# Adding a stored partial result on GpSimd, and taking a row's moments one block later

## The reference, cut to what matters

```python
S = S + eye(n)
Rf = S / S.sum(axis=1)[:, None];  Rb = S / S.sum(axis=0)[:, None]
Xf, Xb, Xa, Z = X, X, X, 0
for s in range(2):
    A = nucleus_softmax(Xa @ W1 @ W2 @ (Xa @ W3).T, p=0.9)   # row-wise top-p
    Xf = Rf @ Xf;  Xb = Rb @ Xb;  Xa = A @ Xa
    Z = Z + (Xf @ U1[s] + Xb @ U2[s] + Xa @ U3[s])
Y = X + Z
out = x + (Y - mean(Y)) / sqrt(var(Y) + 1e-5) * gamma + beta
```

## Time and profile before

| what | value |
|---|---|
| median of three runs | 2001.48 us |
| profiled execution | 1999.62 us |
| its span | 1997.6 us |
| TensorE busy | 1777.0 us (89%) |
| VectorE busy | 1634.1 us (82%) |
| ScalarE busy | 1364.9 us (68%) |
| GpSimd busy | 605.1 us (30%) |
| mean granted TensorE clock | 0.961 |

### The profile page before, as it was taken

One profiled execution on the slowest core, in us unless ns is written; L12 is line 12 of the kernel. 1 busy time (PEld: TensorE's weight loads), 2 busy tenths in 40 slices (PEclk: granted clock), 3 DMA queues, 4 the chain that ended last, 5 costly groups with the idle time before them and its releaser, 6 DMA issues.

```text
span 1997.6 us, 37487 instructions
## 1 busy us (share of the span) xinstructions
PE 1777.0 (89%) x11660; PEld 1312.2 (66%) x11660; DVE 1634.1 (82%) x3964; ACT 1364.9 (68%) x2201; POOL 605.1 (30%) x1056
## 2 busy tenths in 40 slices
PE   4999964899999999993976699999999999999997
PEld 3888832677777777773763466666666676767665
DVE  5444467899999999998864899999999999999987
ACT  5222266888888888983835568686868686777752
POOL 4000131244444444441341132324242323232330
PEclk9999976899999999997988899999999999999998
DMA  6999721454444444442433010101010101010122
GB/s 170 196 202 203 195 100 56 97 117 117 112 105 116 106 111 114 110 108 56 112 77 125 22 42 21 42 21 42 21 42 21 42 21 42 21 41 22 38 91 72
DMA packets 235345, 168.26 MB, mean 84 GB/s; under 512 B 188451, under 2 KB 220577, under 8 KB 235168
## 3 DMA queue, kind: packets, MB, share of 16 engines
q1 hardware_dynamic: 221264, 117.44, 21.6%
q0 software_dynamic: 3744, 22.14, 7.2%
q10 hardware_dynamic: 10288, 28.12, 4.2%
HBM read 107.99 MB, written 37.49 MB: 73 GB/s over the span
## 4 chain that ended last, share of the span: by engine, by line
issue 35%; DVE 21%; PE 19%; POOLq 9%; DVEq 7%; POOL 4%; DMA 2%; ACT 2%; ACTq 0%
DVE probs_t L1588 7%; DVE stats L1595 5%; POOLq L720 5%; PE lg L1165 2%; DMA probs_t<-row_scalars 2%; PE bank L1096 2%; PE bank L1095 2%; PE bank L1079 2%; PE lg L1096 2%; PE lg L1095 2%; PE bank L1200 2%; DVEq L1783 1%; DVE sorted_e L1614 1%; PE bank L1052 1%; DVEq L1612 1%
## 5 line engine op out<-in xcount | busy, mean ns | idle before, releaser
L1188 PE MATMUL bank<-both,s_tile 128*128 128x512 f16 x1352 | 302.4, 381 | 16.9 <-issue 16.9
L1257 PE MATMUL bank<-xcur,probs_t 128*128 128x256 f32 x1352 | 296.1, 379 | 0.0
L1165 PE MATMUL lg<-k_t,q_tile 64*128 64x512 f32 (+1 forms) x820 | 191.6, 568 | 96.1 <-DVE expo L1485 89.1
L1257 PEld LDWEIGHTS bank<-xcur,probs_t 128*128 128x128 f32 x1352 | 255.0, 190 | 33.6
L1188 PEld LDWEIGHTS bank<-both,s_tile 128*128 128x128 bf16 x1352 | 132.8, 98 | 166.7 <-issue 20.0
L1485 DVE TENSOR_SCALAR_CACHE_REDUCE expo<-lg 128x1024 f32 (+1 forms) x208 | 206.8, 1023 | 43.1 <-PE lg L1165 27.4
L660 POOL TENSOR_TENSOR window<-window,probs_t 128x832 f16<-128x832 f32 x104 | 215.2, 2069 | 81.1 <-ACT probs_t L937 68.6
L1165 PEld LDWEIGHTS lg<-k_t,q_tile 64*128 64x128 f32 x820 | 69.3, 192 | 178.6 <-DVE expo L1485 123.1
L868 ACT ACTIVATE expo<-expo,below_max 128x3327 f32<-128x3327 f32 x52 | 159.4, 3065 | 24.7 <-DVE below_max L1493 23.7
L699 POOL TENSOR_TENSOR aims<-found 128x2 f32<-128x2 f32 x26 | 5.1, 195 | 555.6 <-ACT found L903 555.6
L1588 DVE SCALAR_TENSOR_TENSOR probs_t<-expo,mine 128x1664 f32 (+3 forms) x54 | 156.4, 2896 | 8.4 <-issue 8.0
(11 more groups left out here) (303 smaller groups left out, 3628.6 us busy)
## 6 DMA issues: line engine op xcount, KB each, us to landing
s_tile<-s_scratch SPq DMA_DIRECT2D x28, 832.0 KB, 4.5
expo<-in_adj POOLq DMA_DIRECT2D x25, 831.8 KB, 9.7
s_tile<-s_scratch ACTq DMA_DIRECT2D x24, 832.0 KB, 4.5
s_scratch<-s_tile SPq DMA_DIRECT2D x14, 832.0 KB, 10.1
s_scratch<-probs_t SPq DMA_DIRECT2D x6, 832.0 KB, 9.3
s_scratch<-window SPq DMA_DIRECT2D x6, 832.0 KB, 9.6
q_tile<-q_scratch SPq DMA_DIRECT2D x104, 32.0 KB, 2.1
xa_scratch<-ht ACTq DMA_DIRECT2D x26, 128.0 KB, 2.2
```

The costliest lines, as they stand in the source:

```text
L1165: last = T.matmul(lg[c % 2][:, h * CHUNK:h * CHUNK + w], q_tile[b][DA * h:DA * (h + 1), :], k_all[DA * h:DA * (h + 1), s, c0:c0 + w], star ...
L1188: last = T.matmul(s_ps[:, 0:width], s_tile[b][:, k, :], moving, start=(k == 0 and part == 0), stop=(k == NT - 1 and part == 1))
L1257: last = T.matmul(kept_ps[1][:, 0:D], probs_t[:, k * P:(k + 1) * P], xcur[:, k, :], start=(k == 0), stop=(k == NT - 1))
```

## The change

GpSimd gets a new function `add_result`, which adds `y_in` to tile t's result in SBUF; a new semaphore `y_added` counts it. For all tiles but the last, TensorE no longer runs the identity product and ScalarE copies the result out without accumulating. One block later, after its second refinement, ScalarE reads the added result again with a copy that accumulates the row sum, and makes mean and squares there (`added_result`). GpSimd's order becomes: first bracket of tile t+2, centre tile t-1, add tile t. SyncE's load of `y_in` waits for `y_added` instead of `y_done[1]`. The last tile is made as before; in its block ScalarE takes the moments of tile 24 behind the copies L997. `skewed_loop` runs body 0 alone, 22 bodies in a loop, and 3 more alone.

```diff
@@ SyncE, load
-                sp.wait_ge(y_done[1], t + 1)
+                sp.wait_ge(y_added, t + 1)
                 sp.dma_start(y_in[:, :], dram_tile(y_dram, tile_of(m, b))).then_inc(y_loaded[1], DMA)
@@ GpSimd
+            def add_result(t, m, b):
+                y = tile3(y_all, tile_of(m, b))
+                pool.wait_ge(y_out[1], t + 2)
+                pool.wait_ge(y_loaded[1], DMA * (t + 1))
+                G.tensor_tensor(y, y, y_in[:, :], ALU.add).then_inc(y_added, 1)
...
-            with pool.Fori(0, NT // 2 - 1) as i:
-                for b in range(2):
-                    first_bracket(i * 2 + b + 2, i + 1, b)
-                    centre_result(i * 2 + b, i, b)
-            centre_result(NT - 2, NT // 2 - 1, 0)
+            def results(t, m, b):
+                if not (isinstance(t, int) and t >= NT - 2):
+                    first_bracket(t + 2, m + 1, b)
+                if not (isinstance(t, int) and t == 0):
+                    centre_result(t - 1, m - 1 + b, 1 - b)
+                if not is_last(t):
+                    add_result(t, m, b)
+            skewed_loop(pool, results)
@@ ScalarE, step
+                def added_result(t, m, b):
+                    A.activation(turned[:, 0:D], tile3(y_all, tile_of(m, b)), ACT.Copy, accum_out=y_sum[:, :])
+                    result_moments(m, b)
...
                     if is_last(t):
+                        act.wait_ge(y_added, t + 1)
+                        added_result(*before)
                         act.wait_ge(var_ready, 1)
...
+                    if before is not None and not is_last(t):
+                        act.wait_ge(y_added, t + 1)
                     if more:
                         refine(b, 1)
+                    if before is not None and not is_last(t):
+                        added_result(*before)
                     act.drain()
...
-                    A.activation(y, pv_ps[:, 0:D], ACT.Copy, accum_out=y_sum[:, :]).then_inc(y_out[1], 1)
-                    act.drain()
-                    A.activation(mean[:, column], y_sum[:, :], ACT.Copy, scale=-1.0 / D)
-                    act.drain()
-                    A.activation(turned[:, 0:D], y, ACT.Square, bias=mean[:, column], accum_out=var[:, column]).then_inc(y_moments, 1)
+                    if is_last(t):
+                        A.activation(y, pv_ps[:, 0:D], ACT.Copy, accum_out=y_sum[:, :]).then_inc(y_out[1], 1)
+                        result_moments(m, b)
+                    else:
+                        A.activation(y, pv_ps[:, 0:D], ACT.Copy).then_inc(y_out[1], 1)
...
-                    tiles_loop(act, step)
+                    skewed_loop(act, step)
@@ TensorE, step
-                    pe.wait_ge(y_loaded[1], DMA * (t + 1))
-                    T.matmul(pv_ps[:, 0:D], ident[:, :], y_in[:, :], start=True, stop=False)
-                    products(t, True)
+                    if is_last(t):
+                        pe.wait_ge(y_loaded[1], DMA * (t + 1))
+                        T.matmul(pv_ps[:, 0:D], ident[:, :], y_in[:, :], start=True, stop=False)
+                    products(t, is_last(t))
```

More of the change, by code:

```diff
@@ L349, in graph_layers @@
         x_added = sem("x_added")
+        y_added = sem("y_added")
         lo_ready = [sem(f"lo_ready_{n}") for n in range(2)]
@@ L379, in graph_layers @@
             (qk_out, 1),
+            (y_added, 1),
         ]
@@ L990, in first_end, with result_moments @@
                     result_out(t)
+                def result_moments(m, b):
+                    y, column = tile3(y_all, tile_of(m, b)), bass.ds(tile_of(m, b), 1)
+                    act.drain()
+                    A.activation(mean[:, column], y_sum[:, :], ACT.Copy, scale=-1.0 / D)
+                    act.drain()
+                    A.activation(turned[:, 0:D], y, ACT.Square, bias=mean[:, column], accum_out=var[:, column]).then_inc(y_moments, 1)
+                def added_result(t, m, b):
+                    A.activation(turned[:, 0:D], tile3(y_all, tile_of(m, b)), ACT.Copy, accum_out=y_sum[:, :])
+                    result_moments(m, b)
                 def step(t, m, b):
                     more = not (isinstance(t, int) and t >= NT - 2)
+                    before = None if isinstance(t, int) and t == 0 else (t - 1, m - 1 + b, 1 - b)
                     for g, (k0, n) in enumerate(P_GROUPS):
@@ L1017, in step @@
                     act.wait_ge(y_done[1], t + 2)
-                    y, column = tile3(y_all, tile_of(m, b)), bass.ds(tile_of(m, b), 1)
-                    A.activation(y, pv_ps[:, 0:D], ACT.Copy, accum_out=y_sum[:, :]).then_inc(y_out[1], 1)
-                    act.drain()
-                    A.activation(mean[:, column], y_sum[:, :], ACT.Copy, scale=-1.0 / D)
-                    act.drain()
-                    A.activation(turned[:, 0:D], y, ACT.Square, bias=mean[:, column], accum_out=var[:, column]).then_inc(y_moments, 1)
+                    y = tile3(y_all, tile_of(m, b))
+                    if is_last(t):
[3 more added lines that the diff above has]
+                        A.activation(y, pv_ps[:, 0:D], ACT.Copy).then_inc(y_out[1], 1)
                 for t in range(2):
```

## The result

The changed kernel takes 2007.69 us (median of 8 runs, 2006.23 to 2010.26) against 2001.11 us before (8 runs in the same comparison, 1999.64 to 2003.34): ratio 1.0036, 95% interval 1.0028 to 1.0045, which is 5.6 to 9.0 us slower. The forecast was 2007.4 us, slower. The profiled execution took 2007.77 us, its span 2005.7 us, 8.1 us more than before.

A forecast was written before the change was run, and what follows sets the result against it. VectorE, not the 98% busy TensorE, was taken to bound the second pass at 33.8 us a block. Blocks 0 and tail +5.9 on 2001.5 gave 2007.4 us; own range 2004.5 to 2009.5, 8 in 10 within 2001.5 to 2012.

The forecast's parts named there:

- VectorE closes the loop: Second pass: TensorE waits for VectorE's reciprocal L1785 each block, so removing the 0.43 us identity product gains 0.
- the 0.22 us of one block: TensorE's late start in the block shown, waiting for VectorE's reciprocal L1785; forecast to grow to 0.65 us.
- ScalarE's moments in the block cost nothing: Behind the second refinement: 1.46 to 1.65 us of work delays L1013 some 0.8 us, products not delayed; cost 0.
- GpSimd's addition is hidden in the blocks: Behind L738: 0.64 us, ending 0.3 us before VectorE's L1493; cost 0, bounds 0 and +0.64 a block.
- that cover: The 0.3 us between the addition's end and VectorE's L1493, called thin; the rival of collisions in each block had 0.14.
- The collision of block 24: Addition behind held-up L738 meets VectorE's small instructions before the last L1785: +0.4 us, bounds 0 and 0.64.
- The tail: After the last block: tile 24's moments come 7.3 us later, +7.7 with the collision; the end moves +5.9 us.
- It starts 1996.8 - 1990.9 = 5.9 us later than now: Program end: the last store, ready at 1992.6, waits for large stores filling all engines until 1996.8; end +5.9 us.
- on an engine that has just come free: Last store before the change: claimed to leave at 1989.9 and start about 1990.9, large stores having filled engines until 1989.1.
- The sum: Whole kernel: blocks 0, tail +5.9 us; span 2003.5, profiled execution 2005.5, median 2007.4.

The follow-up runs named there:

- e3: Kernel before without the identity product for tiles 0 to 24, nothing added in its place: 2000.23 us against 1999.76, ratio 1.0008.
- e4: Kernel before with the identity product made three times for tiles 0 to 24: 2009.83 us against 1999.76, ratio 1.005.
- e5: Changed kernel with GpSimd's addition made twice for each of 25 tiles: 2011.78 us against 2000.12 for the kernel before, ratio 1.0056.
- e2: Kernel before with only tile 24's mean and squares moved behind the last block's copies L997: 2006.78 us against 1999.76, ratio 1.0035.
- e7: Kernel before with the last store of 127 rows cut into 112 and 15: 1995.51 us against 2000.12, ratio 0.9978.
- e11: Kernel before with the last store split and the 25 tiles' stores in five pieces: 1994.58 us against 2000.15, ratio 0.9977.
- e1: Changed kernel with tile 24 made the old way, its moments taken in block 24: 2000.9 us against 1999.76 for the kernel before, ratio 1.0005.
- e6: Changed kernel with three of VectorE's beta additions put ahead of the variance of 25 tiles: 2001.06 us against 2000.12 for the kernel before.

## Why the prediction was right

**VectorE closes the loop: right.** The period forecast at 33.8 us stayed (+0.06 us over 24 blocks), the wait ahead of L1246 was to be 0.65 us and is 0.66 in the block shown, and e3 shows the same with the product alone. The forecast took the 0.22 us of one block for TensorE's whole spare time; e4 shows 0.56, because there is a second wait for VectorE in each block. Nothing hung on it here.

**ScalarE's moments in the block cost nothing: right.** L1043 was forecast 0.8 us later. It starts 1528.07 - 1521.22 = 6.85 us ahead of the transposes, where L1013 had 7.64: 0.79 later. The products didn't wait.

**GpSimd's addition is hidden in the blocks: right**, with 0.33 us to spare, 0.3 forecast. The price of losing that cover was put at up to 0.64 us a block; in e5 it was 0.15. The upper bound was the whole instruction, but one that has started earlier is partly over when the victim comes, and in 7 of 24 blocks nothing was left. One sentence of the working, that a single-input VectorE instruction beside GpSimd's costs nothing, isn't borne out: L1824 has one tensor input. In the kernel before it took 0.50 us and ended at 1965.31, just behind GpSimd's L736 (below, to 1965.27); in the changed kernel it started ahead of GpSimd's next instruction and took 0.18.

```profile
1964.66 0.61 POOL L736 TENSOR_TENSOR parts<-parts,moments_of_tile 128x256 f32<-128x256 f32 x1 [23.95 <-ACT turned L1023]
```

**The collision of block 24: right in place, wrong in size and cause.** Forecast +0.4, measured +0.82. GpSimd and VectorE of the changed kernel there:

```profile
1927.09 0.20 POOL L707 TENSOR_TENSOR lead<-lead,ends_c 128x4 f32<-128x4 f32 x1 [0.47 <-issue]
...
1929.63 3.58 POOL L719 TENSOR_TENSOR lead<-lead,left_out 128x4 f32<-128x4 f32 x1
...
1937.74 0.64 POOL L746 TENSOR_TENSOR parts<-parts,k_t 128x256 f32<-128x256 f32 x1
1938.34 4.10 POOL L739 TENSOR_TENSOR parts<-parts,y_tile 128x256 f32<-128x256 f32 x1
```

```profile
1937.06 0.57 DVE L1742 COPY mine<-lead 128x16 f32<-128x16 f32 x1 [3.67 <-POOL lead L734]
1937.71 4.15 DVE L1533 SCALAR_TENSOR_TENSOR scraps<-expo,mine 128x3327 uint8<-128x3327 f32 x1
...
1941.95 0.51 DVE L1547 TENSOR_TENSOR mine<-under,mine 128x1 f32<-128x1 f32 x1
```

and of the kernel before, the same two engines:

```profile
1925.85 0.20 POOL L705 TENSOR_TENSOR lead<-lead,ends_c 128x4 f32<-128x4 f32 x1 [0.15 <-issue]
...
1928.71 3.58 POOL L719 TENSOR_TENSOR lead<-lead,picked 128x4 f32<-128x4 f32 x1
```

```profile
1935.78 0.58 DVE L1711 COPY mine<-lead 128x16 f32<-128x16 f32 x1 [3.31 <-POOL lead L732]
1936.45 3.69 DVE L1502 SCALAR_TENSOR_TENSOR scraps<-expo,mine 128x3327 uint8<-128x3327 f32 x1
```

VectorE waits 0.36 us longer for the lead, and its pass L1533 takes 0.46 us longer: 0.82. The forecast had GpSimd's old instruction held up and the addition behind it on VectorE's small ones. Instead the old one (L746) gets in just as L1533 starts and makes it late, and the addition is the one held up in its place; VectorE's L1547 pays 0.51 us as it did. The lead is late because the long lock now falls on the first of the pair of instructions instead of the second, one more of 0.35 us behind it, and that comes from a stall of 0.47 us ahead of L707, 0.15 before, for which the trace names no releaser. (L719 of the changed kernel is L717 of the kernel before; the pair there is L717 and L719.) The kernels with GpSimd's old loop (e2, e3, e4, e7 and e11) take 32.4 us for this stretch, all with the new one 33.2 or more. That the stall comes from the last blocks now being written out of the loop is a guess: no run told it apart.

**The tail: right.** L1824 was forecast 7.3 us later behind the last reciprocal, and is (7.40 against 0.08, +7.32); e1 and e2 show it from both sides. That the size fits so well leans on the clock: the forecast took the end of the last copies from a profile with the granted clock 0.83, and the changed kernel's has it too; at 1.00 those copies end 0.8 us sooner (e2). The last store was forecast ready at 1992.6; with the 1.3 us that had come before it (0.85, 0.06 and the missing 0.42) that is 1993.9, and it leaves at 1994.0, behind the large ones. What was mis-sized is the step "It starts 1996.8 - 1990.9 = 5.9 us later than now". It counts 1.8 us between the end of the large stores (1989.1) and the start of the last one (1990.9) as slack that the change would eat whole. The last store of the kernel before didn't start "on an engine that has just come free": the engines had been empty since 1989.25, it was issued at 1989.9 and began at about 1990.7, so the gap was 1.4 us. After the change a gap of 0.2 us was left (1998.4 to 1998.6), and the slow start, 3 GB/s in the first microsecond instead of 13, took most of the rest. Of the 1.8 us only 0.95 came back (7.32 - 6.37), which makes the end 0.87 us later than forecast.

**The sum.** Forecast 5.9 us for the span, measured 8.1: 0.85 before the second pass, 0.06 in it, 0.42 of block 24 and 0.87 of the store. That the median, 2007.69, lies 0.3 us from the forecast is partly luck: the profiled run before lay 1.9 us below its median and the one after on its median. By the medians of the comparison the change costs 6.6 us, by the three stretches that it touches 7.25.

## What to carry to other kernels

An instruction taken off an engine that is 98% busy gives nothing when each block of that engine begins with a wait for another; look for the wait before counting the saving. To know how much work the engine could take on, add up all its waits and not the largest one, and take the row of the matmuls, not of the weight load (0.22 us read from one wait, 0.56 there). Work put off by one block is free in the loop and paid at its end, where the last block has no successor: +7.3 us of wait here, and nearly free again once other work was put ahead of the waiting instruction (e6). Compare tails only at the same granted clock. And look at the last transfer of a program: 127 rows in one store cost 5.3 us more than 112 and 15.

## What was not expected of the hardware

A store of 127 rows ran on 0.07 of the engines for over 6 us, at 13 to 25 GB/s; the same rows as 112 and 15 were out within about 0.8 us, at up to 254 GB/s (e7). A store queued behind large ones began about 0.2 us after their last bytes, but with 3 rows in its first microsecond, where it moved 13 when the engines were empty. A VectorE instruction held up by GpSimd shows the time as its own duration (0.46 instead of 0.16 us, 4.15 instead of 3.69), not as idle time, so the waits don't tell of it. TensorE's granted clock over the same 10 us of the tail was 0.83 in some profiles and 1.00 in others with the same instructions and the same wait of 1.83 us ahead of them, and that alone moved the end by 0.8 us.
